# Stacking the last 30 rows of a split product on the partitions of one matmul

## The reference

```
norm_x = ln_weight * x * rsqrt(mean(x*x) + eps)
out    = norm_x @ W_root + bias                      # 1024 -> 286
for r in range(2):                                   # relation of the edge
    out += segment_sum((norm_x[src] @ W_rel[r]) * (type == r), dst) / max(count, 1)
y  = elu(out) @ wo_weight                            # 286 -> 1024, the second map
x1 = layernorm(x + (x + y))
```

## Time and profile before

| what | value |
|---|---|
| runs | 943.1, 943.87, 945.9 us; median 943.87 |
| profiled execution, first to last instruction | 943.8 us |
| busy share PE / DVE / ACT | 94% / 78% / 49% |
| mean granted TensorE clock | 0.979 |
| the stage of the change | from 179 to 213 us of the span |

### The profile page before, as it was taken

One profiled execution on the slowest core, in us unless ns is written; L12 is line 12 of the kernel. 1 busy time (PEld: TensorE's weight loads), 2 busy tenths in 40 slices (PEclk: granted clock), 3 DMA queues, 4 the chain that ended last, 5 costly groups with the idle time before them and its releaser, 6 DMA issues.

```text
span 943.8 us, 18917 instructions
## 1 busy us (share of the span) xinstructions
PE 884.8 (94%) x7117; PEld 646.1 (68%) x7118; DVE 734.1 (78%) x1206; ACT 463.5 (49%) x752; POOL 18.2 (2%) x44
## 2 busy tenths in 40 slices
PE   3659999899998999999999999999999999999996
PEld 2537787645467776776786786687687687678542
DVE  5779998595998777777777777777877877776777
ACT  5754445445565545535535535535544453553811
POOL 1000001000000000000000000000000000000000
PEclk9879999899999999999999999999999999999998
DMA  8101000251202222022022022022112202302302
GB/s 264 40 2 51 1 0 1 98 217 68 90 1 90 90 90 89 2 91 90 0 89 89 0 89 89 12 77 89 47 41 89 84 5 90 112 2 90 112 23 87
DMA packets 30375, 63.43 MB, mean 67 GB/s; under 512 B 1513, under 2 KB 4721, under 8 KB 30321
## 3 DMA queue, kind: packets, MB, share of 16 engines
q1 hardware_dynamic: 30321, 62.71, 18.8%
HBM read 57.52 MB, written 5.18 MB: 66 GB/s over the span
## 4 chain that ended last, share of the span: by engine, by line
PE 78%; DVE 13%; issue 4%; ACT 4%; DVEq 1%; POOL 0%; POOLq 0%; ACTq 0%
PE psP L1055 41%; PE psA L1125 18%; PE psP L853 6%; PE psP L904 5%; PE psA L893 4%; DVE wsplit L1311 2%; PE psP L980 1%; DVE wsplit L1305 1%; PE psA L842 1%; DVE stats L1508 1%; DVE u_mem L1553 1%; DVE p_mem L1355 1%; DVE wsplit L1428 1%; ACT u_mem L614 1%; ACT wsplit L553 1%
## 5 line engine op out<-in xcount | busy, mean ns | idle before, releaser
L1055 PE MATMUL psP<-wsplit,xT 128*128 128x256 f16 x2592 | 296.4, 273 | 3.2 <-ACT vec L741 2.8
L1055 PEld LDWEIGHTS psP<-wsplit,xT 128*128 128x128 f16 x2592 | 254.3, 98 | 37.5 <-issue 3.1
L1125 PE MATMUL psA<-p_mem,c_mem 128*128 128x512 f16 x800 | 175.3, 379 | 0.0
L1055 PE MATMUL psP<-wsplit,x 128*128 128x256 f16 x1296 | 150.3, 273 | 1.7 <-DVE key_mem L1619 1.5
L1125 PEld LDWEIGHTS psA<-p_mem,c_mem 128*128 (+1 forms) x800 | 78.2, 98 | 91.0
L1055 PEld LDWEIGHTS psP<-wsplit,x 128*128 128x128 f16 x1296 | 126.7, 98 | 16.8 <-issue 2.2
L1311 DVE SCALAR_TENSOR_TENSOR wsplit<-stage,sc,wsplit 128x1024 f16<-128x1024 f32 x90 | 114.7, 1278 | 27.1 <-ACT wsplit L564 27.1
L564 ACT ACTIVATE wsplit<-stage,sc 128x1024 f16<-128x1024 f32 x90 | 100.6, 1137 | 15.0 <-DVE sc L1202 9.1
L853 PE MATMUL psP<-p_mem 125*128 125x140 f16 x1125 | 77.7, 231 | 18.0 <-ACT u_mem L578 12.9
L853 PEld LDWEIGHTS psP<-p_mem 125*128 125x128 f16 x1125 | 74.8, 101 | 22.4 <-ACT u_mem L578 8.3
L1584 DVE SCALAR_TENSOR_TENSOR u_mem<-psA,coef,u_mem 128x512 f32<-128x512 f32 x80 | 60.0, 750 | 33.0 <-PE psA L1125 30.9
(11 more groups left out here) (199 smaller groups left out, 802.8 us busy)
## 6 DMA issues: line engine op xcount, KB each, us to landing
stage<-in_L_gnn_weight SPq DMA_DIRECT2D x16, 2048.0 KB, 8.0
stage<-in_L_gnn_w_gate SPq DMA_DIRECT2D x4, 2048.0 KB, 7.9
x_home<-x SPq DMA_DIRECT2D x5, 512.0 KB, 2.6
x<-x_home SPq DMA_DIRECT2D x5, 512.0 KB, 5.5
stage<-in_L_gnn_W_rel SPq DMA_DIRECT2D x4, 572.0 KB, 7.6
x<-in_x SPq DMA_DIRECT2D x1, 2048.0 KB
xT<-in_L_gnn_root SPq DMA_DIRECT2D x1, 2048.0 KB, 9.9
stage<-in_L_gnn_root SPq DMA_DIRECT2D x1, 2048.0 KB, 8.2
```

The costliest lines, as they stand in the source:

```text
L1055: last = nc.tensor.matmul(psP[:, bank, (col + tt) * FB:(col + tt + 1) * FB], lhs[tt](a, c), split_block(n, b)[:, c, :], start=(first and t ...
L1125: last = nc.tensor.matmul(psA[:, (NT * h + t) % 2, :], cnt8[:, r, s, t * P:(t + 1) * P], p_part[h][a][:, s, :], start=(s == 0 and a == 0), ...
```

## The change

The 30 last rows get three copies on the partitions, 32 apart (rows 0, 32 and 64), so that one matmul over 96 rows adds up what three did. The activations hold hi, hi, lo on these rows, the weights hi, lo, hi.

```diff
+FREST = F - (FC - 1) * P
+STACK = 32
...
-            sp.dma_start(st_wo[0:F - (FC - 1) * P, FC - 1, :], wo_d[(FC - 1) * P:F, :]).then_inc(wo_tail_loaded, 16)
+            for n in range(3):
+                sp.dma_start(st_wo[n * STACK:n * STACK + FREST, FC - 1, :], wo_d[(FC - 1) * P:F, :]).then_inc(wo_tail_loaded, 16)
...
-                act.wait_ge(wo_tail_loaded, 16)
+                act.wait_ge(wo_tail_loaded, 48)
...
+            def product_wo(out, t, cols):
+
+                _, hi, lo = unit_weights(U_WO)
+                for c in range(FC - 1):
+                    for a, w in ((0, hi), (0, lo), (1, hi)):
+                        nc.tensor.matmul(out, yT[:, a, c, t * P:(t + 1) * P], w[:, c, cols],
+                                         start=(c == 0 and a == 0 and w is hi), stop=False)
+                return nc.tensor.matmul(out, yT[0:3 * STACK, 0, FC - 1, t * P:(t + 1) * P], hi[0:3 * STACK, FC - 1, cols],
+                                        start=False, stop=True)
...
-                    product(psP[:, n % NT, :], yT, U_WO, t, slice(n % 2 * HALF, (n % 2 + 1) * HALF)).then_inc(wo_full, 1)
+                    product_wo(psP[:, n % NT, :], t, slice(n % 2 * HALF, (n % 2 + 1) * HALF)).then_inc(wo_full, 1)
...
             def wo_low():
                 st, hi, lo = flat_weights(U_WO)
                 dve.wait_ge(wo_hi, 1)
-                stt(lo, st, sc_f[:, scale_col(U_WO, 1), 2:3], hi, ALU.mult, ALU.subtract).then_inc(wo_lo, 1)
+                n, rest = (FC - 1) * D, slice(STACK, 2 * STACK)
+                stt(lo[:, 0:n], st[:, 0:n], sc_f[:, scale_col(U_WO, 1), 2:3], hi[:, 0:n], ALU.mult, ALU.subtract)
+                stt(hi[rest, n:], st[rest, n:], sc_f[rest, scale_col(U_WO, 1), 2:3], hi[rest, n:],
+                    ALU.mult, ALU.subtract).then_inc(wo_lo, 1)
...
                 for t in range(t0, t1):
+                    copies = acc0[:, t, F - FREST + STACK:F - FREST + 3 * STACK].rearrange("p (n k) -> p n k", n=2)
+                    rest = acc0[:, t, F - FREST:F].unsqueeze(1).broadcast_to([P, 2, FREST])
+                    ts(copies[:, :, 0:FREST], rest, -1.0, rows_f[:, 0, 2, t:t + 1], ALU.add, ALU.mult).then_inc(y_copied, 1)
+                dve.wait_ge(y_copied, t1)
+                for t in range(t0, t1):
                     ts(acc0[:, t, 0:F], acc0[:, t, 0:F], -1.0, rows_f[:, 0, 2, t:t + 1], ALU.add, ALU.mult).then_inc(y_ready, 1)
...
             def y_low(t):
                 dve.wait_ge(y_hi, t + 1)
-                tt(yT[:, 1, :, t * P:(t + 1) * P], psA[:, t % 2, 0:FPAD].rearrange("p (c n) -> p c n", c=FC),
-                   yT[:, 0, :, t * P:(t + 1) * P], ALU.subtract).then_inc(y_lo, 1)
+                full, rest, cols = FC - 1, slice(2 * STACK, 3 * STACK), slice(t * P, (t + 1) * P)
+                turned_y = psA[:, t % 2, 0:FPAD].rearrange("p (c n) -> p c n", c=FC)
+                tt(yT[:, 1, 0:full, cols], turned_y[:, 0:full, :], yT[:, 0, 0:full, cols], ALU.subtract)
+                tt(yT[rest, 0, full, cols], turned_y[rest, full, :], yT[rest, 0, full, cols], ALU.subtract).then_inc(y_lo, 1)
```

More of the change, by code:

```diff
@@ L280, in build @@
         y_ready = sem("y_ready")
+        y_copied = sem("y_copied")
         y_turned = sem("y_turned")
@@ L889, in product @@
                 _, hi, lo = unit_weights(i)
-                chunks = FC if i == U_WO else DC
-                for c in part or range(chunks):
+                for c in part or range(DC):
                     for a, w, first in ((0, hi, c == 0), (0, lo, False), (1, hi, False)):
                         last = nc.tensor.matmul(out, lhs[:, a, c, bass.ts(t, P)], w[:, c, cols],
-                                                start=first, stop=(c == chunks - 1 and a == 1))
+                                                start=first, stop=(c == DC - 1 and a == 1))
                 return last
+            def product_wo(out, t, cols):
[6 more added lines that the diff above has]
+                                        start=False, stop=True)
             def raw_product(out, lhs, i, t):
```

## The result

The changed kernel takes 946.72 us (median of 18 runs), the kernel before 944.46 us (18 runs beside them). The ratio is 1.0022, with a 95% interval of 1.0014 to 1.0031: 1.3 to 2.9 us slower. That is under the 0.3% that the prediction called no difference; with this many runs it is clear of none all the same. One run of the changed kernel and two of before that took 1500 us and more are left out of the ratio.

The account below looks back on a forecast made before the run. In this stage DVE and ACT, not TensorE, were taken to bound the kernel. 943.8 us plus 1.75 for DVE and 0.3 for clock gave 945.85, with 0.07 from span to median 945.9 us; range 943.8 to 948.8.

Parts of the forecast that it names:

- Two paths meet at the root: At ACT's root for tile 0, 198.65 us: DVE's statistics and ACT's table load arrive within 0.04 us; delaying either delays it.
- The sum: DVE's added time up to tile 0's root plus y_low(4): 1.25 with free starts, 2.25 with completed ones, 1.75 us taken.
- first elu_end, what comes through: Call for tiles 0 and 1: 0.46 us added, fits in DVE's idle 0.66 us; 0.05 us given for a rest.
- wo_low: DVE's lo of the weights, one instruction split into 2048 and 1024 columns: +0.13 us starting freely, +0.30 if each completes first.
- y_low, each: DVE's lo of the activations, five times, split into 256 and 128 columns: +0.065 us with free starts, +0.23 with completed ones.
- elu_end(2, 4): DVE call for two tiles, with small copies and a wait for them before in-place scaling: +0.46 us, no cover.
- elu_end(4, 5): DVE call for one tile, with a small copy and a wait before in-place scaling: +0.29 us, no cover.
- the rule that the prediction put beside its sum: DVE instructions starting in another group of 32 partitions wait until all earlier ones finish; gives the upper 2.25 us.
- DVE dearer than both ends: Rival: DVE costs more through another wait or code fetched at another place; time above 946.7 us, chance 0.08.
- ACT's path: `y_high(2)` and all behind it on ACT start 0.4 to 0.9 us later, less than DVE; DVE's path sets the root.
- The clock: TensorE's half clock in `root_product(0)` may shift with longer idle times: bounds -1.5 and +3.6 us, +0.3 taken.
- The rival that made the whole product slow: TensorE at 1.2 GHz through nearly all of `root_product(0)`: 3.6 us more, 949.2 us; chance 0.2.

Follow-up runs that it names:

- pe_seven: The kernel before with seven matmuls for nine, leaving out the two lo products of the last 30 rows, nothing else; ratio 0.9998.
- after_nine: The changed kernel with nine matmuls for each half again, first chunk's hi and lo products added twice; 1.3 us above the changed kernel.

## Why the prediction was right, point by point

*DVE and ACT set the stage, the saved matmuls of TensorE are worth nothing.* Shown by `pe_seven` (20.42 for 20.41) and by `after_nine` (22.90 for 22.88). `wo_product(0)` was on the chain, as read, and shortening it only uncovered DVE behind it.

*Two paths meet at the root.* Shown: shortening DVE alone gave 0.01 us, shortening `wo_product(0)` alone nothing, and DVE together with the degree matmuls moved away 1.89.

*The sum.* Forecast 1.75 us at the root and `y_low(4)` together, with ends at 1.25 and 2.25; measured 2.47 + 0.28 = 2.75 in the changed kernel's profile. By its terms, each the distance between two starts in the timeline of the changed kernel, for the same distance before:

```
term                         forecast        measured
first elu_end, what comes through   0.05     0.22   (5.17 for 4.95 us)
wo_low                       0.13 .. 0.30    0.34   (3.66 for 3.32)
y_low, each                  0.065 .. 0.23   0.285 to 0.295  (1.52 and 1.50 for 0.93, two)
elu_end(2, 4)                0.46            0.46   (4.64 for 4.18)
elu_end(4, 5)                0.29            0.29   (2.42 for 2.13)
```

The distances run from the anchor to `wo_low`; from `wo_low` to `y_low(0)`; from `y_low(0)` and from `y_low(2)` to the instruction behind the pair; from the first add of `agg0_add(4)` to the weight scale; and from the last elu step of tile 4 (L1479 of the kernel before) to `y_low(2)`. With four `y_low` up to the root the measured terms add up to the 2.47.

The mechanism was right and two terms were mis-sized. The first is `y_low`: I took the middle between free and completed starts, and completed is the case. By the rule that the prediction put beside its sum it would have been the upper end, 2.25. Even that end was 0.06 us too low each: the two durations are 0.42 + 0.29 = 0.71 us, 0.02 above the forecast, and each piece is followed by a gap of 0.01 to 0.04 us before the next start, so that a `y_low` takes 0.75 to 0.76 us from start to start. The second is the cover of the first `elu_end`. I set 0.46 against DVE's idle 0.66 us and gave 0.05 for TensorE's wait on a bank. It let 0.22 through: idle time of an engine is no full cover where its end moves with the work that is put ahead of it. With 2.75 in the place of 1.75 the prediction's own sum is 946.9, above 946.7, so in the stage it was the rival *DVE dearer than both ends* that came true, with a chance of 0.08.

*ACT's path.* Forecast 0.4 to 0.9 us later, measured 1.60: `y_high(2)` starts 193.29 - 177.99 = 15.30 us behind the anchor for 191.94 - 178.24 = 13.70. The same terms are in it (0.22 + 0.34 + 0.58 + 0.46 = 1.60), and the 0.3 us that TensorE was to give back weren't there: in `pe_seven`, too, `y_high(2)` starts 191.79 - 178.08 = 13.71 us behind the anchor. It stayed below DVE's 2.49 at that point (200.62 - 177.99 for 198.38 - 178.24), so the conclusion held: ACT waited 0.87 us, just under the 0.9 to 2 that were forecast.

*The base.* I set the span of 943.8 against the median of 943.87 as if they were one. The changed kernel's profiled execution took 946.5 us for a span of 944.7, so 1.8 us lie around that span, and the span of 943.8 belongs, by an estimate from this, to an execution of about 945.6, near the slowest of the three runs (945.9). As a difference the forecast stands all the same: 2.1 us were measured (1.3 to 2.9), 2.0 forecast. That the two are so near is partly luck. The 2.0 were 1.75 of stage and 0.3 of clock, of which the first was 1.0 us too low in the profile and the second a guess; with the 2.75 that the profile shows and the same guess, the forecast would have been 3.05, just outside the interval.

*The clock.* +0.3 was a guess between -1.5 and +3.6. Over the fourteen profiles the first `root_product` shows 6.05 or 6.06 us to the next in eight and 6.99 to 7.74 in six. Without filling those six are three of five profiles with the stack and three of six without it. A drop that starts at about 199 to 204 us, in `wo_product(2)`, `wo_product(3)` or the turning ahead of it, stands in four of the five profiles with seven matmuls and no filling, and in none with nine. So TensorE's shorter work and longer idle time go together with this drop, in products that nobody waits for. What the change adds to the chance of a drop in `root_product(0)` stays open: filling TensorE's idle time changed no median beyond its interval. The rival that made the whole product slow didn't come in any profile: the most was 1.7 us.

*Other edits.* The two further transfers are issued at 71.6 us, 1.36 us for three, and are landed 5.2 to 6.3 us later, long ahead of the reader at 143.35. Nothing came of them.

The 2.1 us of the medians against 2.75 of the stage agree within the interval.

## What to carry to other kernels

A chain that runs over TensorE at 78% says nothing about a stage of 30 us: ask, for the one stage, who waits for whom at the point where paths meet, and shorten all paths that meet there or none. Saved matmuls that are paid for with small vector instructions are a bad trade where VectorE is the late engine, and the pieces cost their full length when they start at another partition (here 0.75 us a pair, for 0.53 from partition 0). Measure such a stage as a distance between two instructions in the trace, not by the total: here the distance repeats to 0.02 us, while single runs of the kernel before, but for two far above, lie between 941.8 and 947.2.

## What the runs showed that I had not expected

The places at half clock move from execution to execution of one program. Two profiles of the kernel before differ by 2.3 us in span: 0.9 us ahead of the anchor and 1.5 us at 308 us, where TensorE is at half clock for some 3.5 us in one and not in the other, while the distance from the anchor to the root is the same 20.41. The half clock at 308 us can be read from one distance: the first aggregation of layer 1 (`psA`, L1125 of the kernel before) starts 103.8 us behind the second `root_product` in five of the fourteen profiles, without that half clock, and 105.0 to 105.3 in nine, with it. All six profiles of kernels with the stack are among the nine, with three of the eight others. Whether that is chance or comes with the longer stage stays open.
